# Two decoder layers on one core: one pool of eight PSUM banks, constants filled by VectorE, products of zeros at the start, and a new written-out order

## The chip, the cores and the metric

The kernel runs on one core of a Trainium2 chip. The metric is the device time in microseconds (us) of one execution. The core has TensorE (PE: matrix products, results into PSUM), VectorE (DVE), ScalarE (ACT), GpSimd (POOL) and SyncE (SP, which issues the transfers). Each engine works through its own instructions in their written order and waits for the others by semaphores. PSUM has eight banks of 512 fp32 columns in 128 partitions.

## The reference

Sixteen sequences x of 128 tokens x 128 features pass two layers, each step added to x after a layer norm without weights. `cross` takes its keys and values from `ctx`, also 128 x 128 per sequence.

```
h  = norm(x);  x += causal_attention(h, 16 heads of 8) @ Wo            # self0
h  = norm(x);  x += attention(h, ctx, 8 heads of 64) @ Wo + bo         # cross0
h  = norm(x);  x += round(h / amax(h) * 127) @ ternary(w).T * scales   # ffn
h  = norm(x);  x += causal_attention(h, scores clipped to +-10) @ Wout # self1
h  = norm(x);  x += attention(h, ctx, 16 heads of 64) @ O              # cross1
h  = norm(x);  g = softmax(h @ gate_w + gate_b); keep g >= 0.1, rescale to sum 1
               x += sum over 8 experts of g_e * (h @ W_e + b_e)        # moe
```

All is fp32. Where the kernel needs fp32 accuracy from faster products it cuts an operand into a high and a low part and adds three products.

## The kernel before, in words

The work on each sequence is cut into steps (`all_steps`, line 63), named by stage and step and numbered by sequence: `cross1.t.0#13` turns the weights of the first eight heads of the cross1 attention of sequence 13. A step lies on one engine. For one cross attention and eight heads (a unit) the chain is: `rs` (POOL, reciprocal root of the variance), `nm` (ACT, normalised rows), `xT` (PE, transposed), `xTe` (ACT, copy out of PSUM), `q` and `qe`, `s1` (PE, scores of eight heads, 1024 columns), `mx` (DVE, row maxima), `ex` (ACT, eight exponentials of 128 columns, function `cross_exps`), `rc` (DVE, reciprocal sums), `nz` (POOL, division), `t` (PE, eight transposes), `wT` (ACT, copy), `pv` (PE), `oTe` (ACT), `y` (PE), `res` (DVE, adds to x and takes the next statistics). Self attention is similar, with both units of scores written at once (`s1` or `s2`). `moe.g` is the gate, `moe.e` the experts (1024 columns). The keys (`k`) and values (`v`) of the cross attentions hang on ctx alone and are made up to six and four sequences ahead.

**Order.** No planner runs on the chip. The dictionary `ORDER` holds for each engine a string of two-letter codes, one per step: the order in which the engine does all its steps of all sequences, 721 of them on PE. The sequences are interleaved: while sequence 0 is in a late stage, others are in earlier ones. All of an engine's steps are queued behind each other.

**PSUM.** Steps that write PSUM are of two kinds. Kind X takes one bank, kind S takes two neighbouring banks (1024 columns); self scores take two such pairs. Before, four banks are for X (`X_BANKS`) and two pairs for S (`S_GROUPS`). Class `Plan` (line 258) replays the order with the steps' written costs and gives each step the bank of its kind that comes free first in that replay. This fixes the bank and the semaphore count to wait for (`room`, `room_for_scores`). The bank is free when its reader (`until`) has done all its parts.

**Array division.** `array_parts` tells how a step uses the 128 x 128 array: whole, 64 rows (cross scores), 64 columns (cross `pv`), 32 rows or 32 by 32 (self scores).

**Start.** GpSimd fills the constants (`ident`, `mask[0]`, `s_bound`, `head_rows` and small ones), shapes some by `affine_select`, and counts `consts` up. VectorE, ScalarE and TensorE wait for all of them (`N_CONSTS`) before anything else. VectorE then makes `head_mask` and `ident_b` (`const_b`). SP waits for them between its loads of `b_v` and `more`, to copy the mask into three rotated ones. The loads `e_k` and `e_v` (512 KB each, weights of cross1) are copied by ScalarE (`.hi`) and cut by GpSimd (`.lo`) before the first `cross1.k` and `cross1.v`.

Of the kernel before, what the change touches and what calls it, by code (L numbers as in the profile page):

```python
# [30 lines left out]
X_BANKS, S_GROUPS = 4, 2  # L31
AHEAD = dict(cross0=6, cross1=4)
EARLY = 4


class Step:

    def __init__(self, engine, cost, after, again, bank, until, parts, once):
        self.engine, self.cost, self.bank, self.parts, self.once = engine, cost, bank, parts, once
# [23 lines left out]
def all_steps():  # L63
    steps = {}

    def add(name, engine, cost, after=(), again=(), bank=None, until=None, parts=1, once=False):
        steps[name] = Step(engine, cost, after, again, bank, until, parts, once)
# [40 lines left out]
    def keys_values(L, chunks, k_w, v_w):  # L108
        context = ["ctx0.lo", since("ctx1.lo", EARLY)]
        for c in range(chunks):  # L110
            fill(f"{L}.k.{c}", 660, [*context, f"{k_w}.lo"], f"{L}.ke.{c}", [second_ago(f"{L}.s1.{c}", AHEAD[L])])
            add(f"{L}.ke.{c}", "ACT", 486, [f"{L}.k.{c}"])
        for c in range(chunks):
            fill(f"{L}.v.{c}", 650, [*context, f"{v_w}.lo"], f"{L}.ve.{c}", [ago(f"{L}.pv.{c}", AHEAD[L])])
# [21 lines left out]
    for name, cost in (("x0", 3300), ("first", 300), ("x1", 2300), ("c0", 400), ("b_k", 700), ("b_v", 1300),  # L136
                       ("masks", 2000), ("more", 3300), ("e_k", 1400), ("e_v", 1500), ("x", 1900), ("ctx", 2400), ("self1", 800), ("cross1", 3900), ("moe", 1300)):
        add(f"in.{name}", "SP", cost, once=True)
    add("consts", "POOL", 4150, once=True)
    for name, load, engine, hi, lo in (("ctx0", "c0", "DVE", 530, 610), ("b_k", "b_k", "DVE", 530, 610),  # L140
                                       ("b_v", "b_v", "DVE", 530, 610), ("e_k", "e_k", "POOL", 960, 1900),
                                       ("e_v", "e_v", "POOL", 960, 1900), ("ctx1", "ctx", "POOL", 1400, 2800),
                                       ("m_w", "moe", "POOL", 960, 1900)):
# [17 lines left out]
    add("moe.e", "PE", 1300, ["moe.xl", "m_w.lo"], ["moe.sm"], "S", "moe.ml")  # L161
    add("moe.lg", "DVE", 270, ["moe.g"])
# [21 lines left out]
        "aHaLaJaHa4aOa4a6a6a4a4bqaUa6aQaJbWbWbYbWbWaXaObYaLbYb0b0aHaUb2bYaQaZa6b2aJa1a4b0aXaOaZbab2aLaHb2bcaJ"  # L184
        "aUaQbea1a6b0a6aXaOaLbaaHaJaUaZbcbja1aQblbebna4aXaLa4aOa4baaZa6aHaUa1bcbwbjbyaQbeblbCaJbnbEaXbGbJbaaL"
        "aZbca1bjaHbwbebla6bybna4bQaObCbaaJbSbGa6bUbcaUa4bEbjbwaQbyblbJb6b8beaXcccabnaZbCa6claLaHa1bEbQbjbGbS"
        "chbUbwblcjbJb6byb0cab8cqbaccbnclbQbWcsbSb2aObCbcbWbYbYbGaUbEbUaJaQcqcubwchb6beaXbyb8cacsbJaZb2aLa1a4"
        "cycccjclaHcBcubja4a6bCcCbQblaObabEaJbcbnbSbGaQcGcya6cKaUbUcBcqb0becCb6csbwaXchaLcabyb8bJaHaZcGcjcccl"
        "a1cub2bWbjbWbQaOblbCbYcybnbaaUbEbGbcbYbScqcBbUaQcKaJchb0beb6cCb8aXcjbJbwaZcacscccGaLa1byclcubQbjcKb2"
        "a4aHaObCbSbEblbGbUbaaUbnaJcycqaQcBbccsbJb6aXcachb8cCaZbeaLbwa1cccjbybWclbQcubjaHbWbYbCaObScGbGblbUcy"  # L190
        "b0baaUbnbccBcqaQaJcKcCchbEb6b2becsaXb8caaLbJaZaHbwcjccclcubya4a1bja4b2bYaOblbaaJbQcGbna6cybSaQb0bcbU"
        "chbCaUcBbGbwbEcqbybecjb6cCcaaXa4aLbJaHbCb8aZcsccclbEcKa1cubjbQbWbWaOblcGbSb0bYcybnbaaUb2bUaQcBcKcqbc"
        "cCbGaJbeb6chbYbwaXb8caaLbJaHcscjclaZbycGcca1cub2bjbQa6aObCbSbaa6aJbGblcyaQbUcKbnaUbccqcBbeb0b6bEcCca"
        "chaXb8bJcjcsbwaZccclcGa1bWbycuaLbjbYbWbQaOblaHbaa6b2aJbSaUcybcbnbCaQbUcqcKbGcBbEchbeaXcCaLb0aZcsaOcj"
        "b6b0b0cabwaQb8aUclb2a1ccbycubjcGbYaXblbJaZbacybCa1bccBcqbEbnbecKcCcsbQbachb2bcbSbJcjbwcGbUbjbGbecub6"
        "byblb8cKcaccbCcyclbnbWbQbWbjbGcCcBb0bSchblbUbEcqbnbwcjcsb6bJb8bycGcacccuclbCbYbYcKbwbQbGb0bEcybSchcB"
        "bUcCcjbycqb6cGb8bJbCcacsccclcKcub2bQbEbJcybSbGbUcBchcqcCb6cjcab8bQclccbSbUcscucGb6cqb8cachcccKcyclcj"
        "cBcscCcucGchcqcjcscycBcKcucCcycBcGcKcCcGcK"
    ),
    DVE=(  # L200
        "aEaEaraEataEavaTbpaPbraEaYaTaPa2aYaTaPbfa2aEbhaTaYaPa2bfboaEaYbhaTbuaPbxaEbza2bfbobhaYbNbubKbxa2aEbf"
        "bzbobhbRaTbuaPbVbxbzbNbKaEbfaYcdbobhcmcfbRbua2bVcobxbNbzbKcdbocmbRcfcoaTaPbVbuaEbxcvbfbzaYbhbKa2bNcd"
        "cAcDcmcFcfcvcIcobRaPaTbocLcAcDbVcFbubfcIbxaEaYbhbzbNbKcdcma2cvcfcobRaTbocAaPcDbVcFbubfcLcIaYbhbKbNbx"
        "cda2cmbzcvbRcLcfcoaTaPbVaEcAbocDcFbNbKbuaYaEcIbfa2bxcdbhcmbzbRcvcocfaTbVaPcDcAbocFaEcLcIbubfaYbhbNbK"
        "cdbxcmbzcva2cocfaPbRboaTbucAbVaEcDbxcFbfbzcIaYbhbKbNcdcma2cLcfcvbRcoaTaPbocAbVcDcFcIcLbubfbxaYbhbKbN"
        "cmbzcda2cvcobRaPaTcLbVcAcfcDbobfcFcIbhaYbubNbKbxcdcmbza2cvcfcobRaTaPcAbobVcLcDcFbfaYcIbhbuaPaTbxcma2"
        "cdbzcvcoaYcfbNcAa2cDbKcFbobfcLcIbRbhbubNbKbVbxbfbzcvcLbhcdcmbocfcAbRcocDbucFbVcIbobxbNbzbKcdbucvcmcf"
        "cLbxbRcocAcDbVcFbzcIbKbNcdcmcLcvcfbRcobNbKbVcAcDcFcIbRcmcdbVcocfcvcdcLcmcfcAcDcocFcIcvcAcDcLcFcvcIcD"
# [49 lines left out]
class Plan:  # L258

    def __init__(self, steps):  # L260
# [18 lines left out]
        def begin(engine):  # L279
# [9 lines left out]
            if s.until:  # L289
                times.append(sorted(empty[s.bank].values())[len(s.until) - 1])  # L290
# [1065 lines left out]
```

## Time and profile before

| | us |
|---|---|
| median of three runs (529.69 to 532.6) | 531.2 |
| the profiled execution | 529.94 |
| its span, first to last instruction | 528.2 |

| engine | busy us | share of the span |
|---|---|---|
| PE, products | 497.7 | 94% |
| PEld, weight loads, beside the products | 419.3 | 79% |
| ACT | 441.3 | 84% |
| DVE | 409.2 | 77% |
| POOL | 395.2 | 75% |

The profile is of one execution, and its times run from the first instruction. A group "L1119 PE MATMUL S<-kT_cross,qT_cross" is line 1119, on TensorE, which writes the tile S from the two others. A row of the timeline may merge repeated instructions ("x16"): its first number is the start, its second the length in us. "Idle before" names what released the engine. The last columns of the stage view are the clock granted to TensorE (1.00 is 2.4 GHz, 0.50 is 1.2 GHz) and the load of the transfer engines.

### The profile page before, as it was taken

How to read it: one execution, taken by the hardware profiler on the slowest of the kernel's cores; microseconds unless marked ns; L12 is line 12 of the kernel's file. 1: busy time of each engine (PE TensorE's matmuls, PEld its weight loads, DVE VectorE, ACT ScalarE, POOL GpSimd, SP SyncE). 2: the span in 40 equal slices, each digit the busy share in tenths (PEclk: the TensorE clock that was granted, in tenths of full speed). 3: DMA queues.
4: the chain of work that ended last, by engine and by line, in shares of the span. 5: the costliest groups of instructions: out<-in, count | busy, mean ns of one | idle time of the engine just before them, and what ended most of it. 6: DMA issues, size and time to landing. Idle time of an engine off the chain costs nothing.

```text
span 528.2 us, 15974 instructions
## 1 busy us (share of the span) xinstructions
PE 497.7 (94%) x5490; PEld 419.3 (79%) x5490; DVE 409.2 (77%) x923; ACT 441.3 (84%) x1177; POOL 395.2 (75%) x570
## 2 busy tenths in 40 slices
PE   4998989999999999999999999999999999988884
PEld 2876777777988888788888888888988898777762
DVE  3857778887788987979788897889878887786552
ACT  5987789999888888989899888988978898887831
POOL 5785778787678987888868785898778687776454
PEclk9999999999999999999999999999999999999995
DMA  6800000000000000000000000000000000000000
GB/s 195 327 4 1 1 2 3 2 2 2 2 2 6 3 2 7 8 2 3 7 1 2 4 6 7 1 6 4 6 2 2 7 7 2 6 7 2 6 6 11
DMA packets 6463, 8.96 MB, mean 17 GB/s; under 512 B 1008, under 2 KB 4848, under 8 KB 6384
## 3 DMA queue, kind: packets, MB, share of 16 engines
q1 hardware_dynamic: 6384, 7.94, 4.6%
q8 instruction: 45, 0.74, 0.6%
q14 instruction: 34, 0.28, 0.2%
HBM read 6.50 MB, written 1.05 MB: 14 GB/s over the span
## 4 chain that ended last, share of the span: by engine, by line
PE 70%; POOL 8%; issue 7%; POOLq 6%; ACT 4%; DVE 3%; DVEq 1%; ACTq 0%
PE S L1132 11%; PE S L1119 7%; PE X L1076 7%; PE X L1159 7%; PE X L1187 7%; PE S L1106 5%; POOL diff_cross L672 4%; PE X L1292 2%; PE X L1145 2%; PE X L1198 2%; PE X L1170 2%; PE X L1172 2%; PE X L1171 2%; ACT diff_cross L747 2%; PE X L1178 2%
## 5 line engine op out<-in xcount | busy, mean ns | idle before, releaser
L667 POOL TENSOR_TENSOR w_low_self<-w_self 128x1024 f16<-128x1024 f32 x64 | 120.7, 1896 | 15.8 <-ACT w_self L736 10.9
L672 POOL TENSOR_TENSOR diff_cross<-diff_cross,e_rec_cross 128x1024 f32<-128x1024 f32 x48 | 91.0, 1898 | 24.8 <-DVE e_rec_cross L898 24.5
L747 ACT ACTIVATE diff_cross<-S,row_max_cross 128x128 f32<-128x128 f32 x384 | 103.8, 404 | 4.3 <-DVE row_max_cross L889 3.6
L889 DVE TENSOR_REDUCE row_max_cross<-S 128x8 f32<-128x1024 f32 x48 | 57.9, 1215 | 18.2 <-PE S L1119 17.7
L896 DVE TENSOR_REDUCE e_sum_cross<-diff_cross 128x8 f32<-128x1024 f32 x48 | 58.2, 1213 | 3.9 <-ACT diff_cross L747 3.2
L756 ACT ACTIVATE w_cross<-S 128x1024 f32<-128x1024 f32 x48 | 49.7, 1039 | 8.4 <-PE S L1132 8.0
L1119 PE MATMUL S<-kT_cross,qT_cross 64*128 64x128 f32 x768 | 54.6, 283 | 0.2 <-ACT qT_cross L712 0.2
L1119 PEld LDWEIGHTS S<-kT_cross,qT_cross 64*128 64x128 f32 x768 | 46.4, 187 | 7.3 <-issue 4.5
L1159 PE MATMUL X<-w_cross,v_cross 128*64 128x128 f32 x768 | 51.7, 278 | 0.1
L1132 PE MATMUL S<-ident,diff_cross 128*128 128x128 f32 x384 | 50.3, 274 | 0.9 <-POOL diff_cross L672 0.8
L1159 PEld LDWEIGHTS X<-w_cross,v_cross 128*64 128x64 f32 x768 | 41.1, 136 | 11.0 <-issue 5.7
L1132 PEld LDWEIGHTS S<-ident,diff_cross 128*128 128x128 f32 x384 | 42.8, 141 | 2.8 <-issue 1.1
L916 DVE SCALAR_TENSOR_TENSOR w_self<-S,s_bound 128x1024 f32<-128x1024 f32 x32 | 38.0, 1217 | 5.4 <-PE S L1106 5.4
L907 DVE TENSOR_TENSOR w_self<-S,row_max_self 128x1024 f32<-128x1024 f32 x32 | 39.2, 1225 | 2.4
L905 DVE TENSOR_REDUCE row_max_self<-S 128x8 f32<-128x1024 f32 x32 | 38.9, 1217 | 1.8 <-PE S L1106 1.6
L736 ACT ACTIVATE w_self<-S 128x1024 f32<-128x1024 f32 x32 | 33.0, 1032 | 7.6 <-PE S L1132 7.6
L730 ACT ACTIVATE w_self<-w_self,shift 128x1024 f32<-128x1024 f32 x32 | 36.8, 1148 | 2.8 <-DVE w_self L916 2.8
L1106 PE MATMUL S<-by_head_self,plain_self 32*128 32x512 f32 x256 | 36.5, 640 | 1.8 <-ACT by_head_self L712 1.8
L712 ACT ACTIVATE by_head_self<-X,head_mask 128x128 f32<-128x128 f32 x128 | 37.3, 402 | 0.0
L1076 PE MATMUL X<-xnT_cross,e_q 128*128 128x128 f32 x256 | 33.7, 279 | 0.7 <-issue 0.4
L1132 PE MATMUL S<-ident,w_self 128*128 128x128 f32 x256 | 33.6, 274 | 0.5 <-DVE w_self L907 0.4
L1187 PE MATMUL X<-e_o,attnT_cross 128*128 128x128 f32 x256 | 32.1, 278 | 1.5 <-issue 1.4
(191 smaller groups left out, 1396.7 us busy)
## 6 DMA issues: line engine op xcount, KB each, us to landing
out_dram<-x_all SPq DMA_DIRECT2D x16, 64.0 KB, 1.5
x_all<-in_x SPq DMA_DIRECT2D x1, 768.0 KB, 7.3
cT_all<-in_ctx SPq DMA_DIRECT2D x1, 768.0 KB, 9.0
e_k<-in_e_k SPq DMA_DIRECT2D x1, 512.0 KB, 4.9
e_v<-in_e_v SPq DMA_DIRECT2D x1, 512.0 KB, 6.0
e_q<-in_e_q SPq DMA_DIRECT2D x1, 512.0 KB, 9.0
e_o<-in_e_o SPq DMA_DIRECT2D x1, 512.0 KB, 11.3
m_w<-in_m_w SPq DMA_DIRECT2D x1, 512.0 KB, 9.0
```

Source lines behind the costliest of these rows:

```text
L667: pool.tensor_tensor(L.w_low[u][:], L.w[u][:], halves(L.w[u][:]), ALU.subtract)\
L672: pool.tensor_tensor(L.diff[u][:].rearrange("p (h k) -> p h k", h=UNIT), L.e[u][:].rearrange("p (h k) -> p h k", h=UNIT), L.e_rec[:, u, :] ...
L747: last = act.activation(L.e[u][:, P * p:P * (p + 1)], S_[:, P * p:P * (p + 1)], ACT.Exp, bias=L.row_max[:, u, p:p + 1])
L756: act.activation(L.w[u][:], group(i, turn)[:], ACT.Copy).then_inc(taken(i, turn)[0], 1)
L889: dve.tensor_reduce(L.row_max[:, u, :], group(i, turn)[:].rearrange("p (h k) -> p h k", h=UNIT), AX_X, ALU.max, negate=True).then_inc(L.ma ...
L896: dve.tensor_reduce(L.e_sum[:, u, :], L.e[u][:].rearrange("p (h k) -> p h k", h=UNIT), AX_X, ALU.add)
L1076: last = pe.matmul(bank(i, name)[:, P * k:P * (k + 1)], w[:, col:col + P], xT, start=True, stop=True)
L1106: last = pe.matmul(group(i, name, u)[:, 512 * half:512 * (half + 1)], L.plain[rows, :], L.by_head[rows, :, :].rearrange("p j n -> p (j n)" ...
L1119: last = pe.matmul(S_[:, at:at + P], L.qT[rows, h // 2, :], kT[rows, h // 2, i % 2, :], start=True, stop=True)
L1132: last = pe.transpose(S_[:, P * k:P * (k + 1)], L.diff[u][:, P * k:P * (k + 1)], ident[:])
L1159: last = pe.matmul(bank(i, name)[rows, P * pair:P * (pair + 1)], v[:, h, :], L.w[c][:, P * place(h):P * (place(h) + 1)], start=True, stop= ...
L1187: last = pe.matmul(bank(i, name)[:, 0:P], L.attnT[:, c, :], w(c), start=c == 0, stop=c == n - 1)
```

## The change

1. The eight banks are one tensor `psum`. A step of kind X takes any bank, one of kind S any two neighbours; the replay chooses those that come free first, X counting from bank 0 up and S from the top down. Each reader step has a semaphore of its own (`used_up`), and a wait that an earlier one has already covered is left out.
2. `cross_exps` counts its semaphore up after four and after eight exponentials, and the first of the two banks may be handed on after the first count.
3. VectorE fills the constants. GpSimd waits for the first four fills (`blank`), does its selections in another order and waits for all constants. VectorE waits for them behind its first statistics.
4. Before its wait for the constants, TensorE does nine products of zeros (128 x 128 by 128 x 512, bf16) into the last bank.
5. All strings of `ORDER` are new but SP's. Some written costs are changed; the consts step's goes from 4150 to 2700.

```diff
-X_BANKS, S_GROUPS = 4, 2
+BANKS = 8
+WARM = 9
-            fill(f"{L}.k.{c}", 660, ...
+            fill(f"{L}.k.{c}", 710, ...
-            fill(f"{L}.v.{c}", 650, ...
+            fill(f"{L}.v.{c}", 695, ...
-            add(f"{L}.ex.{c}", "ACT", 2060, [f"{L}.mx.{c}"], [f"{L}.t.{c}"])
+            add(f"{L}.ex.{c}", "ACT", 2060, [f"{L}.mx.{c}"], [f"{L}.t.{c}"], half=1030)
-    add("moe.e", "PE", 1300, ...
+    add("moe.e", "PE", 1385, ...
...
+        def choose(s, asked):
+            chosen, gone = [], set()
+            for _ in s.until:
+                places = range(BANKS) if s.width == 1 else range(BANKS - 2, -1, -1)
+                places = [p for p in places if not gone & {p, p + s.width - 1}]
+                since, at_ = min(((max([asked] + empty[p:p + s.width]), n) for n, p in enumerate(places)),
+                                 default=(math.inf, 0))
+                p = places[at_] if places else 0
+                gone |= set(range(p, p + s.width))
+                chosen.append((since, list(range(p, p + s.width))))
+            return chosen
...
             pool side:
-            pool.memset(ident[:], 0.0)
-            pool.memset(mask[0][:], 0.0)
-            pool.memset(s_bound[:], CLIP * SD ** 0.5)
-            pool.memset(head_rows[:], 1.0)
-            pool.drain()
+            pool.wait_ge(blank, 4)
             pool.affine_select(out=ident[:], ...
...
             cross_exps:
-                last.then_inc(taken(i, turn)[0], 1)
+                    if p % 4 == 3:
+                        last.then_inc(taken(i, turn)[0], 1)
...
             VectorE, in self0.st of sequence 0, after the statistics:
+                        dve.wait_ge(consts, N_CONSTS)
+                        dve.tensor_reduce(head_mask[:], ...).then_inc(const_b, 1)
+                        dve.tensor_copy(ident_b[:], ident[:]).then_inc(const_b, 1)
             and ahead of all its steps:
-            dve.wait_ge(consts, N_CONSTS)
+            dve.memset(ident[:], 0.0).then_inc(blank, 1)
+            dve.memset(head_rows[:], 1.0).then_inc(blank, 1)
+            dve.memset(mask[0][:], 0.0).then_inc(blank, 1)
+            dve.memset(s_bound[:], CLIP * SD ** 0.5).then_inc(blank, 1)
+            dve.memset(weighted[:, 4:8, :], 0.0).then_inc(still_ready, 1)
+            dve.memset(eps[:], LN_EPS)
...
             TensorE:
+            def room(i, name):
+                for j, user, half in plan.before[i, name]:
+                    count = use_count(j, user, half)
+                    if waited.get(user, 0) < count:
+                        pe.wait_ge(used_up[user], count)
+                        waited[user] = count
...
+            pe.wait_ge(still_ready, 1)
+            for _ in range(WARM):
+                pe.matmul(psum[:, 512 * (BANKS - 1):512 * BANKS], still[:, 0:P], still[:, 0:512], start=True, stop=True)
             pe.wait_ge(consts, N_CONSTS)
```

Two passages of the order that the prediction speaks of. PE from its first step on: before `xT#0 v#0 qk#0 xT#1 cross0.k.0#0 self0.s1#0`, after `xT#0 v#0 qk#0 cross0.k.0#0 cross0.k.0#1 cross0.k.0#2 xT#1 self0.s1#0` (self0's steps where no stage is named). ACT near the end: before `cross1.ex.0#13 cross1.ex.1#13 self1.qke#15`, after `cross1.ex.0#13 self1.qke#15 cross1.ex.1#13`.

## Rows read from the trace of the kernel before

**Rows 1.** The page, part 1: busy us (share of the span) and instructions.
```profile
PE 497.7 (94%) x5490; PEld 419.3 (79%) x5490; DVE 409.2 (77%) x923; ACT 441.3 (84%) x1177; POOL 395.2 (75%) x570
```
**Rows 2.** Busy us by stage: PE, PEld, DVE, ACT, POOL, clock, DMA, GB/s.
```profile
35.00:125.00 90.00, 84.34 (x950) 67.27 (x949) 69.35 (x145) 76.81 (x201) 69.30 (x105) 1.00 0.01 2
125.00:450.00 325.00, 324.37 (x3704) 279.02 (x3702) 271.60 (x619) 289.37 (x788) 253.93 (x360) 1.00 0.02 4
450.00:500.00 50.00, 44.06 (x491) 36.31 (x490) 35.00 (x81) 40.33 (x115) 32.93 (x42) 1.00 0.02 6
500.00:529.00 29.00, 17.51 (x113) 13.42 (x113) 12.59 (x48) 8.05 (x24) 14.44 (x20) 0.79 0.03 8
```
**Rows 3.** Timeline of the start: start us, length us, what.
```profile
0.92 0.53 POOL L609 MEMSET mask<- 128x512 bf16 x1
1.53 0.11 POOL L611 MEMSET head_rows<- 128x16 f32 x1
...
3.35 0.20 POOL L622 TENSOR_SCALAR_AFFINE_SELECT head_rows<-head_rows 128x16 f32<-128x16 f32 x1
4.04 0.16 POOL L631 MEMSET v_self<- 128x32 f32 x1
...
5.08 0.19 POOL L638 TENSOR_TENSOR var_eps_self<-mean_var_self,eps 128x1 f32<-128x1 f32 x1 [0.89 <-DVE mean_var_self L860]
7.15 0.45 PE L1292 MATMUL X<-ident,xn_self 128*128 128x128 f32 x1 [7.15 <-ACT xn_self L762]
```
**Rows 4.** Timeline of TensorE in the middle, and its last cross1.xT.
```profile
202.06 1.16 PE L1119 MATMUL S<-kT_cross,qT_cross 64*128 64x128 f32 x16
203.16 0.33 PE L1292 MATMUL X<-ident,xn_cross 128*128 128x128 f32 x1
...
299.18 1.09 PE L1159 MATMUL X<-w_cross,v_cross 128*64 128x128 f32 x16
300.20 2.06 PE L1119 MATMUL S<-kT_cross,qT_cross 64*128 64x128 f32 x32
302.19 0.71 PE L1198 MATMUL X<-xnT_self,d_qk 128*128 128x128 f32 x4
...
355.89 1.97 PE L1159 MATMUL X<-w_cross,v_cross 128*64 128x128 f32 x32
357.79 0.33 PE L1292 MATMUL X<-ident,a_unit 128*128 128x128 f32 x1
...
489.52 0.33 PE L1292 MATMUL X<-ident,xn_cross 128*128 128x128 f32 x1 [0.27 <-ACT xn_cross L762]
```
**Rows 5.** Transfers: size, us from issue to landing.
```profile
x_all<-in_x SPq DMA_DIRECT2D x1, 64.0 KB, 2.0
e_k<-in_e_k SPq DMA_DIRECT2D x1, 512.0 KB, 4.9
```
**Rows 6.** Timeline of TensorE, products of 256 columns, early and late.
```profile
10.10 0.42 PE L1171 MATMUL X<-cT_all_lo,b_k_hi 128*128 128x256 f32 x1
10.32 0.41 PE L1172 MATMUL X<-cT_hi,b_k_hi 128*128 128x256 f32 x1
...
156.28 0.28 PE L1171 MATMUL X<-cT_all_lo,b_k_hi 128*128 128x256 f32 x1
156.40 0.28 PE L1172 MATMUL X<-cT_hi,b_k_hi 128*128 128x256 f32 x1
```
**Rows 7.** Timeline: issue of e_k, its low part, its first product.
```profile
10.57 0.43 SPq L595 DMA_DIRECT2D e_k<-in_e_k  x1
...
16.81 2.39 POOL L559 TENSOR_TENSOR e_k_lo<-e_k,e_k_hi 128x1024 fp32r<-128x1024 f32 x1 [0.52 <-ACT e_k_hi L773]
19.42 0.36 PE L1170 MATMUL X<-cT_hi,e_k_lo 128*128 128x256 f32 x1
```
**Rows 8.** Timeline of ScalarE near the end.
```profile
465.35 4.25 ACT L747 ACTIVATE diff_cross<-S,row_max_cross 128x128 f32<-128x128 f32 x16
```
**Rows 9.** Waits, 450 to 500 us: us in total, times, longest.
```profile
PEld S L1106 <- ACT by_head_self L712: 1.8, 1, 1.8
```

More of the change, by code:

```diff
@@ L64, in all_steps, with add @@
     steps = {}
-    def add(name, engine, cost, after=(), again=(), bank=None, until=None, parts=1, once=False):
-        steps[name] = Step(engine, cost, after, again, bank, until, parts, once)
+    def add(name, engine, cost, after=(), again=(), bank=None, until=None, parts=1, once=False, half=0):
+        steps[name] = Step(engine, cost, after, again, bank, until, parts, once, half)
     def fill(name, cost, after, until, again=(), parts=1, once=False):
@@ L189 @@
[L189 to L193, printed above, removed]
@@ L306, in __init__ @@
             ended[i, name] = now + cost + TAIL[engine]
-            for k in range(len(s.until)):
-                b = min((since, b) for b, since in empty[s.bank].items())[1]
-                empty[s.bank][b] = math.inf
-                self.bank[i, name, k] = b
-                self.turn[i, name, k] = (turns[s.bank][b], turns[s.bank][b] + s.parts)
-                turns[s.bank][b] += s.parts
+            self.before[i, name] = []
+            for k, (_, chosen) in enumerate(choose(s, now)):
+                self.banks[i, name, k] = chosen
+                for b in chosen:
+                    if last[b]:
+                        self.before[i, name].append(last[b])
+                    empty[b] = math.inf
             if name in gives:
                 taken, k = gives[name]
-                empty[steps[taken].bank][self.bank[i, taken, k]] = ended[i, name] + HOP[engine]["PE"]
+                for z, b in enumerate(self.banks[i, taken, k]):
+                    half = s.half and z == 0
+                    empty[b] = now + (s.half if half else cost) + TAIL[engine] + HOP[engine]["PE"]
+                    last[b] = i, name, bool(half)
         self.end = max(ended.values())
@@ L436, in bank @@
         def bank(i, name):
-            return X[plan.bank[i, name, 0]]
+            b = plan.banks[i, name, 0][0]
+            return psum[:, 512 * b:512 * (b + 1)]
         def gates(i, k):
@@ L443, in group, with use_count @@
         def group(i, name, k=0):
-            return S[plan.bank[i, name, k]]
+            b = plan.banks[i, name, k][0]
+            return psum[:, 512 * b:512 * (b + 2)]
+        def use_count(i, user, half=False):
+            s = plan.steps[user]
+            if s.half:
+                return 2 * i + (1 if half else 2)
+            return readers[user] * (i + 1)
+        readers = {u: s.parts for s in plan.steps.values() for u in s.until}
         def emptied(i, name):
-            return x_free[plan.bank[i, name, 0]], plan.turn[i, name, 0][1]
+            user = plan.steps[name].until[0]
+            return used_up[user], use_count(i, user)
         def taken(i, name, k=0):
-            return s_free[plan.bank[i, name, k]], plan.turn[i, name, k][1]
+            user = plan.steps[name].until[k]
+            return used_up[user], use_count(i, user)
         x_all = sb("x_all", [P, NSEQ, P])
@@ L1083, in self_scores1 @@
                 pe.wait_ge(*emptied(i, f"{L.name}.qk"))
-                room_for_scores(i, name, 2)
+                room(i, name)
                 if i == 0:
```

171 lines of the change are left out of this document (85 added, 86 removed).

## The prediction

> **What bounds the kernel now.** I read the page's engine table first, then the busy time by stage, the start times of TensorE's products, the start of the timeline, and the waits last. The page puts TensorE's products at 94% of the span and the other engines between 75% and 84% [rows 1], so TensorE is the bound, with little room around it. By stage the reader is to see a middle (125 to 450 us) with 324.4 us of 325 busy, a filling stretch before it (35 to 125) with 5.7 us of 90 idle, and a drain from 450 with 17.4 us of 79 idle [rows 2]; in front lies a start whose first product comes at 7.15 [rows 3].
>
> Busy time hides short gaps, because a product's end is modelled and overlaps the next start. So I counted from start to start. On an undisturbed TensorE a step costs about: keys 0.71 and values 0.72 us (48 each), cross projection 0.89 (48), cross scores 1.0 (48), a turn of eight blocks 0.87 (80), weights times values 0.92 (48 cross) and 0.81 (32 self), self scores 1.29 and 0.92 (16 each), experts 1.47 (16), cross output 0.89 and 1.77 (16 each), the 289 small steps together 51. The sum is 452 us. Each change of the array's division (whole, 64 rows, 64 columns, 32 rows) adds about 0.1: a cross score group that stands alone takes from 202.06 to 203.16, 1.10 us, while two together take 300.20 to 302.19, 1.99 instead of 2.20; a group of weights times values alone takes 299.18 to 300.20, 1.02, and two take 355.89 to 357.79, 1.90 instead of 2.04 [rows 4]. Joining two groups saves two changes, so one is worth 0.07 to 0.105. PE's order string holds 204 of them, 21 us. TensorE thus has 473 us of work in a span of 528.2. The lag (start of a step minus the work that stands before it in the order) tells where the rest goes: it is 9.7 us at 35 us, 22.7 at 123, 30.9 at 451, and 50 at TensorE's end, 523, with 5 of tail behind. Filling costs 13 us, the middle 8, the drain 19.
>
> The Trainium skill would read more headroom into the middle. Its page "Perfetto Trace Analysis", section "Identifying the Most-Contended Engine", says that matmul busy time is a bad measure of the distance to the limit and that the busy share of weight loads is one to use; by that the middle stands at 86% (279.0 of 325 us), and an order could win up to 45 us there. The values above, which repeat step after step, say that only 8 are to be had. I go by the starts.
>
> **The change, part by part.** The profiled execution took 529.9 us for a span of 528.2 and lies 1.3 us under the median of 531.2. The terms are worked out on it and carried over to the median.
>
> *Constants by VectorE.* Today GpSimd makes all of them and the last ends at 4.20; its first reciprocal root starts at 5.08, the first product at 7.15. After, VectorE clears four tiles; GpSimd ended the same four at 1.64, I take 1.7. GpSimd's selections ended at 3.55 [rows 3], so they should end at 3.4. VectorE's other fills lie beside them: one of 512 columns at 0.53 (the mask's row), two of 128 columns and seven tiny ones at about 0.9 together, done near 3.1. The first statistics no longer wait for constants but for x, 2.0 us from issue to landing [rows 5], about 3.0. GpSimd can then start near 3.75 instead of 5.08, and the first transposed product could start at 5.8. The wait for all constants now stands in VectorE's queue behind the first statistics and holds the second ones and the cuts; the cuts wait for ScalarE's copies anyway, so it costs nothing. Were the constants made in another order than I think, it costs up to 0.5.
>
> *Products of zeros.* TensorE has nothing else before 5.8. The granted clock is printed as 1.00 from the start, but the early products run at the lower of the two levels, 1.2 GHz: 256 columns are 0.22 us apart at 10.10, and 0.12 apart at 156.28 [rows 6]. TensorE had worked from 7.15 before it rose, near 11.3. At 1.2 GHz nine products of 512 columns take 9 x 0.43 = 3.9 us. They start when VectorE has filled their operand, near 2.4, and end at 6.3: that is half a microsecond after the first real product could come, so that one starts at 6.3 and not 7.15. In exchange the key products before the first scores cost 0.71 and not 1.4 us. The key weights should be cut at 8.9; three key steps then lie before the first scores, which start at 11.2 as now, but with 3.3 us of work done instead of 1.75. The lag falls by 1.5. If the zeros do not raise the clock it falls by 0.5; at best, with data alone as the limit, by 2.5.
>
> *New order at the start.* Much of this meets a load. e_k lands 4.9 us after its issue [rows 5], which is at 10.57, so at 15.5; its low part is ready at 19.20, and the first product with it starts at 19.42 [rows 7]: 0.2 us of cover. SP's wait ahead of the mask copies ended with the constants at 4.20 and had just begun then (its issues before it fill its queue to 4.0), so e_k leaves only 0.2 us earlier and its low part is ready at about 18.9. The new order has 10.5 us of work ahead of it, not 9.75, so the lag there is 8.4 against 9.7. I take **1.3 us** for the whole start (0.3 to 2.5).
>
> *New order, changes of division.* The new string holds 185 against 204. 19 x 0.1 = **1.9 us** (1.3 to 2.0 by the two pairs), all on the bounding engine.
>
> *One pool; a score group's first bank handed on at half time.* ScalarE reads a cross score group in eight activations, 2.1 us (sixteen in 4.25 [rows 8]); the first four free one bank after 1.05. It can then take any single product, and turns, scores and experts can use any two neighbours. TensorE's work stays the same. The 48 more increments lie on ScalarE, which idles 36 us in the middle [rows 2]; I price them at nothing, and at 48 x 0.1 = 5 us at most if that idle time were gone. How much of TensorE's stall is waiting for banks the trace does not tell apart; the whole stall of the middle is 8 us, so the gain there is 0 to 6. The new step costs for keys, values and experts (710, 695, 1385 ns instead of 660, 650, 1300) stand nearer to the measured 710, 720 and 1470, so the planned times by which banks are dealt out drift less. I take **0.5** for the middle, and **1.0** of the 13 in filling (minus 4 to plus 6: the order is new throughout and nothing in the trace fixes it).
>
> *New order, drain.* One stall can be named: the last self scores wait 1.8 us for ScalarE, which stands in sixteen exponentials from 465.35 to 469.6 ahead of copying that sequence's queries and keys [rows 8, 9]. In the new order eight of them come after. From the last cross1.xT on (489.52 [rows 4]), 21.8 us of work are left in both orders under a chain of 38.7 us, so nothing is won there. I take **1.3** (minus 1 to plus 5).
>
> Sum: 1.3 + 1.9 + 0.5 + 1.0 + 1.3 = 6.0 us. 529.9 becomes 523.9, and the median of 531.2 becomes **525.2**.
>
> **Rivals.** (a) *Only what can be counted comes:* the start is eaten at e_k (0.3), the changes give 1.9, everything else returns as other stalls: 529.0. For it: filling and drain are latency of one sequence's chain over four engines, which banks do not shorten. (b) *The order is much better:* filling and drain give 5 and 4 us, the middle 1.5, the start 2, the changes 1.9, together 14.4: 516.8. For it: 32 us of stall outside the middle; against it: the untouched tail. (c) *Slower, by pairs of banks.* Scores had two pairs of their own. Now a pair is free only when both neighbours are, and one bank can be held long: the gate's until VectorE has normalised its weights. The dealing follows planned times, so a late reader stops TensorE with everything queued behind. A pair is taken 176 times; if each waits 0.07 us more on average, 12 us are lost beside the 6 won: 537. From 0.034 us each on, nothing is won. Against it: the other engines idle 11 to 22% in the middle and so keep near the plan [rows 2]. (d) *The change does not do what it says:* zeros do not raise the clock, and the order only moves stalls: 531.
>
> **How the numbers follow.** Chances: forecast 0.46, (a) 0.20, (b) 0.13, (c) 0.13, (d) 0.08. A difference under 0.5%, 2.7 us, cannot be told from none here. Faster (under 528.5): the forecast's 0.46, four tenths of (a), all of (b), together 0.67. Slower: most of (c), 0.12. Within: the rest, 0.21. The range of 518 to 532 leaves out half of (b) and most of (c), 0.17; the forecast's own range is 521.5 to 528.5.
>
> **What the profile after would show.** Nine products of zeros from about 2.4, 0.43 apart; the first real product near 6.3, and key products 0.12 apart from the first one on. The first product with e_k's low part at 18.9. A lag of 8.4 us at 35, 20.4 at 123 and 28.1 at 451, over 471 us of work. No wait over 0.5 us of the last self scores for ScalarE. I am wrong if score steps in the middle stand behind long waits for one bank's last reader, if the zeros end after 7.15, or if the chain from the last cross1.xT to the end grows beyond 38.7 us.

## The result and the profile after

| us | before | after |
|---|---|---|
| median of four runs each | 530.73 (529.69 to 532.6) | 517.82 (516.53 to 520.02) |
| the profiled execution | 529.94 | 516.53 |
| its span | 528.2 | 514.5 |

The ratio is 0.976, interval 0.974 to 0.979: 12.9 us less, where 6.0 were forecast (5.5 against this median). The time is 7.4 us under the forecast and 0.2 us under the range. Rival (b), "the order is much better", had said 516.8.

Part 1 of the page of the changed kernel, the line that answers to [rows 1]:
```profile
PE 491.8 (96%) x5499; PEld 417.4 (81%) x5499; DVE 409.7 (80%) x937; ACT 440.0 (86%) x1177; POOL 393.6 (77%) x557
```
TensorE's busy time fell by 5.9 us although nine products came in; the other engines do what they did. By stage, as [rows 2]:
```profile
35.00:125.00 90.00, 86.98 (x1040) 70.37 (x1037) 72.55 (x150) 80.80 (x217) 70.07 (x105) 1.00 0.01 2
125.00:450.00 325.00, 323.36 (x3707) 281.10 (x3706) 276.07 (x639) 291.30 (x794) 260.13 (x369) 1.00 0.02 4
450.00:500.00 50.00, 44.95 (x490) 38.98 (x489) 33.81 (x85) 38.44 (x105) 32.62 (x41) 1.00 0.02 6
500.00:529.00 29.00, 5.53 (x18) 3.29 (x16) 5.30 (x17) 1.89 (x7) 6.79 (x11) 0.80 0.02 5
```
The reader is to see two things. In filling TensorE starts 1040 products where it started 950. And after 500 us 5.5 us of products are left instead of 17.5: by then the kernel is 12 us ahead. The middle shows next to nothing by busy time, so the lag (start of a step minus the work ahead of it in its own order) is taken again, for both kernels at the first step from 35, 124 and 452 us on. The last stretch holds all that is left of the span.

| us | before | after | gain | forecast |
|---|---|---|---|---|
| lag at 35 | 9.7 | 9.0 | 0.7 | 1.3 |
| filling, 35 to 124 | 13.0 | 8.5 | 4.5 | 1.0 |
| middle, 124 to 452 | 8.6 | 6.2 | 2.4 | 0.5 |
| drain and tail | 23.8 | 19.5 | 4.3 | 1.3 |
| work with changes of division | 473.1 | 471.3 | 1.8 | 1.9 |
| span | 528.2 | 514.5 | 13.7 | 6.0 |

The steps themselves cost what they cost before (a turn 0.873 us in both middles, an experts step 1.47); the work differs by the 19 changes alone. The 1.8 us for them are those 19 at the cost that the rows of before give for one, about 0.1 us; no run measures them by themselves.

The start after, on three engines, in the columns of [rows 3]:
```profile
0.88 0.17 DVE L1085 MEMSET ident<- 128x128 f32 x1 [0.88 <-PEq L1391]
...
1.07 0.27 DVE L1087 MEMSET mask<- 128x256 uint32 x1
...
2.08 4.02 PE L1350 MATMUL psum<-weighted 128*128 128x512 bf16 x9 [2.08 <-DVE weighted L1089]
...
3.56 0.19 POOL L661 TENSOR_TENSOR var_eps_self<-mean_var_self,eps 128x1 f32<-128x1 f32 x1 [0.23 <-DVE mean_var_self L884]
...
5.89 0.42 PE L1331 MATMUL psum<-ident,xn_self 128*128 128x128 f32 x1
...
6.77 0.46 PE L1246 MATMUL psum<-a_v,xnT_self 128*128 128x128 f32 x2 [0.46 <-ACT xnT_self L735]
...
8.80 0.36 PE L1209 MATMUL psum<-cT_hi,b_k_lo 128*128 128x256 f32 x1 [1.12 <-DVE b_k_lo L590]
...
9.00 0.28 PE L1210 MATMUL psum<-cT_all_lo,b_k_hi 128*128 128x256 f32 x1
9.12 0.28 PE L1211 MATMUL psum<-cT_hi,b_k_hi 128*128 128x256 f32 x1
```
The zeros start at 2.08, GpSimd's first root at 3.56, the first real product at 5.89 and the first key product at 8.80, and behind that first one the key products are 0.12 apart, where they were 0.22 apart before [rows 6]: the higher clock is there. The low part of e_k is met as foreseen, 0.4 us earlier than before [rows 7]:
```profile
16.49 2.36 POOL L590 TENSOR_TENSOR e_k_lo<-e_k,e_k_hi 128x1024 fp32r<-128x1024 f32 x1 [4.03 <-ACT e_k_hi L797]
...
18.98 0.36 PE L1209 MATMUL psum<-cT_hi,e_k_lo 128*128 128x256 f32 x1
```
The end: TensorE's last cross1.xT, which stood at 489.52 [rows 4], and from the view of waits from 450 to 500 us the wait that answers to [rows 9]:
```profile
477.01 0.27 PE L1331 MATMUL psum<-ident,xn_cross 128*128 128x128 f32 x1
```
```profile
PEld psum L1145 <- ACT by_head_self L735: 0.9, 1, 0.9
```
From the last cross1.xT to the end it is 37.5 us against 38.7. The named wait fell from 1.8 to 0.9. ScalarE's sixteen exponentials in one piece [rows 8] are gone. The same two groups, of sequence 13, now have the queries and keys of sequence 15 between them, and stand some 10 us earlier:
```profile
455.10 2.18 ACT L770 ACTIVATE diff_cross<-psum,row_max_cross 128x128 f32<-128x128 f32 x8
457.12 0.33 ACT L735 ACTIVATE plain_self<-psum 128x128 f32<-128x128 f32 x1
457.29 1.19 ACT L735 ACTIVATE by_head_self<-psum,head_mask 128x128 f32<-128x128 f32 x4
458.29 2.25 ACT L770 ACTIVATE diff_cross<-psum,row_max_cross 128x128 f32<-128x128 f32 x8
```

### The profile page after: what moved, and what is told of

Same layout as the page of the kernel before. It is cut to its first block, busy times and chain, and to the rows that moved or that the text cites. A ratio compares the mean times of both kernels' runs of the same rounds, so it can differ in the third digit from the quotient of the medians.

```text
span 514.5 us, 15998 instructions
## 1 busy us (share of the span) xinstructions
PE 491.8 (96%) x5499; PEld 417.4 (81%) x5499; DVE 409.7 (80%) x937; ACT 440.0 (86%) x1177; POOL 393.6 (77%) x557
## 4 chain that ended last, share of the span: by engine, by line
PE 77%; ACT 7%; issue 4%; DVE 4%; POOLq 3%; POOL 3%; DVEq 1%; DMA 0%; ACTq 0%
PE psum L1171 12%; PE psum L1158 9%; PE psum L1198 8%; PE psum L1226 8%; PE psum L1115 8%; PE psum L1145 5%; PE psum L1184 3%; PE psum L1331 2%; PE psum L1237 2%; ACT diff_cross L770 2%; PE psum L1217 2%; PE psum L1186 2%; PE psum L1218 2%; PE psum L1219 2%; PE psum L1209 2%
## 5 line engine op out<-in xcount | busy, mean ns | idle before, releaser
L770 ACT ACTIVATE diff_cross<-psum,row_max_cross 128x128 f32<-128x128 f32 x384 | 104.5, 410 | 7.9 <-DVE row_max_cross L913 7.4
L913 DVE TENSOR_REDUCE row_max_cross<-psum 128x8 f32<-128x1024 f32 x48 | 58.0, 1218 | 17.8 <-PE psum L1158 17.7
L780 ACT ACTIVATE w_cross<-psum 128x1024 f32<-128x1024 f32 x48 | 49.9, 1049 | 6.0 <-PE psum L1171 5.1
L1158 PE MATMUL psum<-kT_cross,qT_cross 64*128 64x128 f32 x768 | 53.2, 282 | 0.5 <-ACT qT_cross L735 0.3
L1198 PEld LDWEIGHTS psum<-w_cross,v_cross 128*64 128x64 f32 x768 | 41.1, 136 | 15.4 <-issue 13.7
L1198 PE MATMUL psum<-w_cross,v_cross 128*64 128x128 f32 x768 | 51.3, 278 | 0.3 <-issue 0.2
L1158 PEld LDWEIGHTS psum<-kT_cross,qT_cross 64*128 64x128 f32 x768 | 46.0, 187 | 6.4 <-issue 4.2
L1171 PE MATMUL psum<-ident,diff_cross 128*128 128x128 f32 x384 | 49.3, 273 | 0.4 <-ACT by_head_self L735 0.3
L1171 PEld LDWEIGHTS psum<-ident,diff_cross 128*128 128x128 f32 x384 | 42.7, 141 | 1.7 <-ACT by_head_self L735 0.5
L931 DVE TENSOR_TENSOR w_self<-psum,row_max_self 128x1024 f32<-128x1024 f32 x32 | 39.2, 1225 | 2.4
```

What stands on the lines that cost most here:

```text
L770: last = act.activation(L.e[u][:, P * p:P * (p + 1)], S_[:, P * p:P * (p + 1)], ACT.Exp, bias=L.row_max[:, u, p:p + 1])
L780: act.activation(L.w[u][:], group(i, turn)[:], ACT.Copy).then_inc(taken(i, turn)[0], 1)
L913: dve.tensor_reduce(L.row_max[:, u, :], group(i, turn)[:].rearrange("p (h k) -> p h k", h=UNIT), AX_X, ALU.max, negate=True).then_inc(L.ma ...
L1158: last = pe.matmul(S_[:, at:at + P], L.qT[rows, h // 2, :], kT[rows, h // 2, i % 2, :], start=True, stop=True)
L1171: last = pe.transpose(S_[:, P * k:P * (k + 1)], L.diff[u][:, P * k:P * (k + 1)], ident[:])
L1198: last = pe.matmul(bank(i, name)[rows, P * pair:P * (pair + 1)], v[:, h, :], L.w[c][:, P * place(h):P * (place(h) + 1)], start=True, stop= ...
```

## The experiments

Theory: the gain is the new order, and it comes only with the banks and the dealing for which that order was laid out. Rivals: the pool by itself gives it; the start gives it; the order gives it whatever the banks are. The last could not be tried directly: the new order asks for more banks at once than four single ones and two pairs offer (replayed with those, it comes to a stop), so an order was searched for those banks instead (below). Times are medians, ratios are to the kernel before in the same job (530.4 to 531.0 us), with 95% intervals.

| kernel | banks | order | start | us | ratio |
|---|---|---|---|---|---|
| after | pool, half | new | new | 517.8 | 0.976 |
| e1 | pool, half | old | new | 537.5 | 1.012 [1.009, 1.015] |
| e5 | pool, half | old | old | 536.0 | 1.011 [1.008, 1.014] |
| e6 | 4 and 2 pairs | old | new | 532.3 | 1.003 [1.002, 1.005] |
| e3 | pool, half | new | old | 517.4 | 0.974 [0.972, 0.977] |
| e8 | pool, no half | new | new | 532.9 | 1.004 [1.002, 1.006] |
| e9 | pool, half, dealt by the old costs | new | new | 523.1 | 0.986 [0.984, 0.989] |
| e10 | 4 and 2 pairs | searched | new | 526.8 | 0.992 [0.989, 0.995] |
| e15 | 4 and 2 pairs | e10's | 11 zeros more | 525.0 | 0.990 [0.988, 0.991] |
| e12 | pool, half | searched | new | 520.9 | 0.982 [0.980, 0.983] |
| e14 | pool, half | e12's | 11 zeros more | 518.5 | 0.977 [0.976, 0.979] |
| e11 | pool, no half | searched | 5 zeros more | 517.8 | 0.976 [0.975, 0.978] |
| e16 | pool, half | new | 5 zeros more | 516.8 | 0.974 [0.973, 0.976] |

The same account of the lag, each from one profiled execution:

| us | lag at 35 | filling | middle | drain, tail | work | span |
|---|---|---|---|---|---|---|
| e1 | 9.2 | 15.7 | 8.4 | 27.0 | 473.1 | 533.4 |
| e5 | 11.5 | 16.6 | 8.5 | 24.5 | 473.1 | 534.2 |
| e6 | 11.1 | 12.9 | 9.0 | 24.1 | 473.1 | 530.2 |
| e3 | 11.4 | 8.7 | 5.7 | 18.5 | 471.3 | 515.6 |
| e8 | 10.3 | 9.8 | 18.1 | 22.4 | 471.3 | 531.9 |
| e9 | 11.1 | 9.1 | 10.3 | 20.0 | 471.3 | 521.8 |
| e15 | 12.7 | 9.3 | 6.5 | 21.6 | 472.6 | 522.7 |
| e11 | 9.7 | 7.7 | 7.0 | 19.6 | 471.2 | 515.2 |
| e16 | 9.6 | 8.4 | 6.4 | 18.8 | 471.3 | 514.5 |

### The old order over the new banks

e1 is the changed kernel with the strings of before; e5 has the old start as well. Both deal the banks by the new costs.

```diff
-        "aHaLaJa4a4a4aHaOa4a6a6a6a6aQaJbqaUbYbYbWbYbYaX...
+        "aHaLaJaHa4aOa4a6a6a4a4bqaUa6aQaJbWbWbYbWbWaXaO...
```

> The kernel after with the order strings of before; pool, half-time hand-on, fills by VectorE, zeros and new costs kept. Theory A (the new order makes the gain; the pool only allows it): 528 to 531 us, the 1 to 2 us of the start are all that is left. Rival B (the pool frees TensorE from bank waits in any order): 519 to 522. By A the lag (start of a TensorE step less the work before it) goes from 9.7 at 35 us to over 21 at 123, by B to 18.

> Order and start of before, the pool of eight banks, half-time hand-on and new costs alone. Theory A: no gain, 530 to 532 us. Rival B: 520 to 523 us. If it is slower than 534, the dealing of banks by planned times does harm by itself under an order that was not laid out for it.

Measured: 537.5 and 536.0, both slower than before by more than their intervals. Without its order the pool does not help: the kernel is 5 to 6.5 us slower, about the 537 of rival (c) of the prediction. Part of it is that rival's mechanism, waits for banks, in filling. TensorE's waits from 35 to 125 us (waited for, total, times, longest), first the kernel before, then e1:
```profile
PE X L1217 <- DVE attn_self L934: 0.8, 2, 0.4
```
```profile
PE psum L1145 <- DVE attn_self L958: 1.9, 1, 1.9
PE psum L1171 <- ACT diff_cross L770: 1.2, 1, 1.2
```
The first row is the largest item of the kernel before in this stretch. In e1 self scores wait once, 1.9 us, for VectorE to have read another step's output (`attn_self`), and a turn of weights 1.2 us for the exponentials of a score group: neither uses the waiting step's own data, so what they wait for is a bank. The middle loses nothing (8.4 against 8.6).

Another part is the clock. The last self scores of e1 come behind a wait of 1.62 us for their own data, about the wait that the kernel before has at the same place. In e1 the granted clock falls to 0.50 there, from 474.6 to 481.4 us; before, it does not. In e5 it falls from 82.7 to 86.1, at the end of the bank wait of 1.95 us. The same eight score products, first in the kernel before, then in e1 and e5:
```profile
470.85 1.14 PE L1106 MATMUL S<-by_head_self,plain_self 32*128 32x512 f32 x8 [1.64 <-ACT by_head_self L712]
```
```profile
474.06 1.64 PE L1145 MATMUL psum<-by_head_self,plain_self 32*128 32x512 f32 x8 [1.62 <-ACT by_head_self L735]
```
```profile
82.83 2.09 PE L1141 MATMUL psum<-by_head_self,plain_self 32*128 32x512 f32 x8 [1.95 <-DVE attn_self L969]
```
At the lower level the products take nearly twice as long (2.09 us for 1.14). By estimate, 6.8 us at that level cost e1 up to 3.4 us, as much as its drain loses (27.0 against 23.8), and 3.4 us of it cost e5 up to 1.7 of the 3.6 us that its filling loses. So what banks alone cost the old order is shown for filling only, 2.7 us in e1. The rest of the 5 to 6.5 us is in good part lost clock, in one case behind a bank wait and in the other not.

### The new order without the hand-on at half time, and with the old dealing

```diff
e8:
-            add(f"{L}.ex.{c}", "ACT", 2060, ..., half=1030)
+            add(f"{L}.ex.{c}", "ACT", 2060, ...)
-                    if p % 4 == 3:
-                        last.then_inc(taken(i, turn)[0], 1)
+                last.then_inc(taken(i, turn)[0], 1)
e9:
-            fill(f"{L}.k.{c}", 710, ...
+            fill(f"{L}.k.{c}", 660, ...
-            fill(f"{L}.v.{c}", 695, ...
+            fill(f"{L}.v.{c}", 650, ...
-    add("moe.e", "PE", 1385, ...
+    add("moe.e", "PE", 1300, ...
```

> The kernel after with one edit: a cross score group's two banks are handed on together, after its eighth exponential. Order and pool stay; the banks are dealt out anew. Theory A2 (order and bank dealing fit each other; an order in banks it was not laid out for loses): 523 to 532 us. Rival D (the order's steps are good in themselves, and one bank a microsecond later is small): 518 to 520 us.

> The kernel after, but the banks are dealt out by the old costs of keys, values and experts (660, 650, 1300). Only bank numbers and the waits for them change. Theory A2: 520 to 524 us, since a dealing by other times sends steps to banks whose reader is late. Rival D: 517 to 519 us, no change.

e8 gives back all of the gain, 15.1 us over after, with 48 increments fewer to do. 12 of its 17.4 us of span are lost in the middle, where busy time now shows it (up to 1.7 of the 12, by estimate, are a fall of the clock from 127.8 to 131.2, behind a wait of 1.75 us for exponentials):
```profile
125.00:450.00 325.00, 315.39 (x3580) 271.30 (x3578) 265.07 (x606) 281.45 (x763) 248.96 (x355) 0.99 0.02 4
```
One such place in the timeline of e8, the experts of sequence 0:
```profile
151.34 0.24 DVE L896 TENSOR_TENSOR moe_lo<-psum,moe_hi 128x128 fp32r<-128x128 f32 x1
...
153.54 2.19 ACT L770 ACTIVATE diff_cross<-psum,row_max_cross 128x128 f32<-128x128 f32 x8
...
153.73 0.39 PE L1301 MATMUL psum<-m_g,moe_xnT 128*128 128x8 f32 x2
...
155.87 0.47 PE L1312 MATMUL psum<-m_w_hi,moe_lo 128*128 128x512 f32 x1 [1.75 <-ACT diff_cross L770]
```
The experts' data (`moe_lo`) have been there since 151.58. TensorE does the gate at 153.73 and then stands for 1.75 us until the eight exponentials of another sequence have read their two banks. In the changed kernel the same two steps follow each other:
```profile
146.85 0.39 PE L1302 MATMUL psum<-m_g,moe_xnT 128*128 128x8 f32 x2
147.09 0.48 PE L1313 MATMUL psum<-m_w_hi,moe_lo 128*128 128x512 f32 x1
```
e9 changes no instruction of the work, only which bank each step gets (157 of 721 differ) and the waits for them, and costs 5.3 us. Of the 7.3 us of its span, 4.1 are in the middle (10.3 against 6.2) and 2.1 before 35 us, where self scores stand for a bank whose reader is late:
```profile
PE psum L1130 <- DVE attn_self L958: 1.6, 1, 1.6
```
Costs of three kinds of steps that are 45 to 85 ns lower are enough for that.

### The start

e3 is the changed kernel with the start of before. e6 has the new start under the old order and the old kinds of banks. It is not the new start alone: it deals the banks by the new costs, and in the replays of the two kernels 331 of the 721 banks taken come from another step than before.

```diff
-WARM = 9
+WARM = 0
-            pool.wait_ge(blank, 4)
+            pool.memset(ident[:], 0.0)
+            pool.memset(mask[0][:], 0.0)
+            ...
```

> The kernel after with the start of before: GpSimd makes all constants, every engine waits for them first, no products of zeros. Theory A: the start gives what is still there at 35 us, 0.65 us of lag, and what later stages keep of it: 518 to 520 us. Rival C (the early start is carried through to the end and multiplies, since each engine's chain of sequence 0 begins earlier): 521 us or more.

> Order of before, four single banks and two pairs as before, no half-time hand-on; only the start of after (fills by VectorE, zeros) and the reader's semaphores. Theory A: 529 to 530.5 us. Rival C: 527 or less. My prediction's term for the start was 1.3 us: 529.4.

e3 takes 517.4 (517.2 to 517.4 in four runs): in the median the new start gives nothing (0.5 us the other way, inside the intervals). Its profiled lag at 35 us is 2.4 higher than after's, as a start without zeros should be. Of that 1.0 comes back in the drain (18.5 against 19.5), and its executions are all alike, while those of after spread over 3.5 us: it is 0.3 to 0.8 us slower than after's two short ones. e6 is 1.3 us slower than before, and whether by its start or by its dealing stays open. TensorE's timeline in e6:
```profile
2.08 4.02 PE L1349 MATMUL psum<-weighted 128*128 128x512 bf16 x9 [2.08 <-DVE weighted L1088]
5.90 0.42 PE L1330 MATMUL psum<-ident,xn_self 128*128 128x128 f32 x1
7.74 0.77 PE L1245 MATMUL psum<-a_v,xnT_self 128*128 128x128 f32 x2 [1.42 <-ACT xnT_self L735]
...
9.88 0.42 PE L1209 MATMUL psum<-cT_all_lo,b_k_hi 128*128 128x256 f32 x1
10.10 0.41 PE L1210 MATMUL psum<-cT_hi,b_k_hi 128*128 128x256 f32 x1
...
14.04 0.28 PE L1209 MATMUL psum<-cT_all_lo,b_k_hi 128*128 128x256 f32 x1
14.16 0.28 PE L1210 MATMUL psum<-cT_hi,b_k_hi 128*128 128x256 f32 x1
```
The same nine zeros, at the same time. Here the key products are still 0.22 apart at 10.10 and the rise comes at 14.0, later than near 11.5 in the kernel before, without zeros. Between the zeros and the keys TensorE waited 1.42 us for a copy (0.46 in after). That alone does not decide it: e1, with the same start, the same first steps and a wait of 1.25 us at the same place, is at the higher clock from 7.0 on:
```profile
7.56 0.46 PE L1246 MATMUL psum<-a_v,xnT_self 128*128 128x128 f32 x2 [1.25 <-ACT xnT_self L735]
...
9.61 0.28 PE L1210 MATMUL psum<-cT_all_lo,b_k_hi 128*128 128x256 f32 x1
9.72 0.28 PE L1211 MATMUL psum<-cT_hi,b_k_hi 128*128 128x256 f32 x1
```
Nor is the time of the rise fixed without zeros: e5 starts with the same products as the kernel before, within 0.02 us, and its clock rises at 14.4, not 11.5. In ten of the eleven kernels with zeros at the front the clock rises at 4.9 to 8.1 us, in the three without them at 11.5 to 14.4. So zeros at the front mostly bring the early rise, but not each time, and why e6 missed it stays open.

### Orders searched for other banks

To see whether the old banks could have had this gain, orders were searched: neighbouring steps exchanged in the engines' strings, kept where a replay with the given banks and step costs becomes shorter. e10 is for four banks and two pairs with whole groups and was searched from the old order; e12, for the pool with the hand-on at half time, and e11, for the pool with whole groups, were searched from the new one. They are three finds of such a search, not the best orders there are.

```diff
e10, e15:
-                places = range(BANKS) if s.width == 1 else range(BANKS - 2, -1, -1)
+                places = range(4) if s.width == 1 else (6, 4)
e10, e15, e11:
-            add(f"{L}.ex.{c}", "ACT", 2060, ..., half=1030)
+            add(f"{L}.ex.{c}", "ACT", 2060, ...)
e14 and e15 (11), e11 and e16 (5), behind sequence 0's v and qk:
+                    for _ in range(11):
+                        pe.matmul(psum[:, 512 * (BANKS - 1):512 * BANKS], still[:, 0:P], still[:, 0:512], ...)
all but e16: new strings in ORDER
```

> Four single banks and two pairs as before, no half-time hand-on, start and new costs of after, and an order of my own: searched from the old one by moving single steps, for exactly these banks. 198 changes of division. Theory A3 (a better order is not to be had without the pool): 525 to 530 us. Rival E (before was just badly searched, the pool is not needed): 517 to 521 us.

> The kernel after with my own order, searched from its order with start-to-start costs as measured in the trace (keys 714, values 712, experts 1465, self scores 1285 and 920, a change of division 95 or 150 ns). 194 changes. If order and costs are what counts (A2), it beats after: 508 to 514 us. If not (D), 516 to 520.

Both came out with a cold stretch at the start. TensorE in e12:
```profile
6.68 0.61 PE L1237 MATMUL psum<-xnT_self,a_qk 128*128 128x128 f32 x4
9.80 0.66 PE L1130 MATMUL psum<-mask,ident_b 32*32 32x512 bf16 x16 [2.51 <-DMA mask<-mask]
10.39 2.09 PE L1145 MATMUL psum<-by_head_self,plain_self 32*128 32x512 f32 x8
...
15.14 0.38 PE L1209 MATMUL psum<-cT_hi,b_k_lo 128*128 128x256 f32 x1
15.35 0.28 PE L1210 MATMUL psum<-cT_all_lo,b_k_hi 128*128 128x256 f32 x1
```
The queries and keys of sequence 0 ran at the higher level (0.61 us for four products, as in after). Then TensorE waits 2.5 us for the copied mask, as this order has no key steps to do before the scores. The granted clock falls at 8.5, and the scores take 2.09 us where e16 needs 1.14. The clock is back at 15.3. In e10 it is back at 19.0, and its runs spread from 523.3 to 527.8. So zeros were put into that gap, and the question of the banks was asked again with this disturbance gone:

> e12_search_costs with eleven more products of zeros (0.22 us each at the upper clock level) on TensorE behind sequence 0's first v and qk, where that kernel idled 2.5 us; its clock had risen at 5.1 us, fallen at 8.5 and risen again only at 15.3. Theory F (my searched order lost to after by the clock of its first 15 us, not by its order): 516.0 to 518.0 us, 3 to 4 less than e12. Rival G (it lost by bank waits all along): 520 to 521 us.

> e10_search_split (four single banks and two pairs, order searched for them) with the same eleven products of zeros; its clock rose for good only at 19.0 us. Theory A3 (the pool is needed for the rest): 521 to 524 us. Rival E (before was only badly searched): 517 to 519 us.

> Pool of eight banks, groups handed on whole, an order searched for exactly that from after's order, and five more products of zeros in the first gap. e8, the same banks under after's order, took 532.9 us. Theory A2 (an order fitted to its banks is what counts; the half-time hand-on itself is small): 518 to 522 us. Rival H (the half-time hand-on is itself worth most of the 15 us that e8 lost): 527 us or more.

e15, the best found for the old banks, is 5.5 us faster than before. e11 and e14, for the pool, are 12.7 and 12.1 us faster. So at least 5.5 us of the gain are order that the old banks could have had. The other 7 are at most what the pool adds, for e10's search began at another order than e11's. The account says where they lie (e15 against e11): 3.0 up to 35 us, 1.6 in filling, 2.0 in the drain, 1.4 in fewer changes of division, and nothing in the middle. The 3.0 up to 35 us need not be the banks' doing: the kernel before, with the same kinds of banks, has a lag of 9.7 there, as e11 has, against e15's 12.7. That leaves about 4 us that the pool may be needed for, which is argued from the account, not shown by a run. e11 also settles the hand-on at half time. Taken away under an order that counts on it, it costs 15 us; with an order made for whole groups, at most 1 us is missing (517.8, against 517.8 of the changed kernel and 516.8 of e16, which has e11's five more zeros).

### The changed kernel with five more zeros

> The kernel after with five more products of zeros behind sequence 0's first v and qk, in its idle stretch from 7.7 to 8.8 us. Its four runs had been 516.5, 517.0, 518.6 and 520.0 us, the first two with a mean clock of 0.991, the others 0.983 to 0.985. Theory F: all executions now have the early clock, 516.3 to 517.3 us with less spread. Rival: the spread is not the clock's, 517.8 us as after, or 0.3 more by the added products.

516.8 us (516.55 to 517.08 in four runs), against 516.5 to 520.0 without them. It is the fastest kernel here by median, 1.0 us under after, though the two ratios' intervals overlap (0.973 to 0.976, 0.974 to 0.979), and none of its four executions was one of the longer ones. TensorE's timeline in e16:
```profile
8.10 1.24 PE L1333 MATMUL psum<-weighted 128*128 128x512 bf16 x5
9.13 0.36 PE L1209 MATMUL psum<-cT_hi,b_k_lo 128*128 128x256 f32 x1
9.33 0.28 PE L1210 MATMUL psum<-cT_all_lo,b_k_hi 128*128 128x256 f32 x1
...
11.92 1.14 PE L1145 MATMUL psum<-by_head_self,plain_self 32*128 32x512 f32 x8
```
They push the first key product from 8.80 to 9.13 and raise the lag at 35 us by 0.6. In exchange, so far as the times tell, the clock is kept in all four.

## Why the prediction was wrong

*Right.* The bound, TensorE, and where its stall lay. Every step's own cost is unchanged, and the changes of division are the 19 that were counted. The start in its single times: root at 3.56 (3.75), first real product 5.89 (6.3), keys at 8.8 (8.9) and 0.12 apart, first use of e_k's low part at 18.98 (18.9). The named wait, under 1 us if not under the 0.5 I set. None of the three signs of being wrong appeared (the zeros ended before 7.15, the chain at the end shrank to 37.5 us, no score step of the middle stood long for a bank), and the forecast was wrong all the same: they watched for a loss, and what was missed is a gain.

*Wrong, the sizes of three terms.* Filling was taken at 1.0 and gave 4.5; drain at 1.3 and gave 4.3; the middle at 0.5 and gave 2.4. The step that failed is the one by which they were priced. I took pool, half-time hand-on, costs and order as separate edits, looked for a row that shows each one's stall, found one (1.8 us), and put a small number on what no row shows. The runs show that they are one edit: the same new order gives 12.9 us with its banks and its dealing, 7.3 with the old dealing (e9) and minus 2.5 without the hand-on (e8), and the same pool gives minus 5 to minus 6.5 with the old order (e1, e5). A sum over the parts, each priced by itself, does not give 12.9. The lag shows it by place: 8.4, 20.4 and 28.1 us were foreseen at 35, 123 and 451, and 9.0, 17.5 and 23.7 came.

*Wrong, the reason against.* For rival (a) I wrote that filling and drain are latency of one sequence's chain, which banks do not shorten. Filling fell by a third. Even the order searched for the old banks has 9.3 us of it for 13.0, and the one searched for the pool 7.7. The stall was the interleaving, which an order can change, and only the last part was chain: from the last cross1.xT on 1.2 us are won, as foreseen (nothing). The other 3.1 of the drain come before that product: the lag at it was 38.2 (7 more than at 452) and is 27.5 (4 more), by the same 21.8 us of work behind it.

*Wrong, what the start is worth.* The single times were right, and the lag at 35 us shows 0.7 instead of 1.3. But e3 without any of it is as fast in the median. The prediction took the rise as something that the zeros bring. In the traces the same nine zeros are followed by a rise at 4.9 to 8.1 us in ten kernels and at 14.0 in an eleventh, so it mostly came; but a clock that has risen can fall again behind a wait (e1, e5, e8, e10, e12). The two longer executions of after have a lower mean granted clock, 0.985 and 0.983 against 0.991 in the two short ones. For the longest, a mean lower by 0.008 over 518 us is some 8 us more at 0.50 instead of 1.00, which costs about 4 us by estimate, and it is 3.5 us longer: the clock accounts for its length. Where that clock was lost no trace shows. That no such execution came with five more zeros speaks for the start; four executions are few, and in e1, e5 and e8 the falls lie elsewhere.

*The rivals.* (b) came, with sizes near its own (filling 5, drain 4, middle 1.5, changes 1.9) but for the start (2). The one thing against it was the untouched tail, and from the last cross1.xT on only 17 of the 55 us of stall are lost, so its chance of 0.13 was low for the reason given. (c) is real in its mechanism: bank waits in filling under the old order (e1), and the experts' wait in e8. Its size of 5 us and more is reached under the old order only together with lost clock. What keeps it away in the changed kernel is that the order was laid out with the banks (e9, e8). Of (d), zeros that do not raise the clock are seen in e6's first 14 us alone.

What stays open: how the gain would divide under the best orders for each set of banks, since the searched ones are finds from different beginnings, and how often the clock is lost in each kernel, since there is one trace of each.

## What to carry to other kernels

When a written-out order and the buffers under it change together, price them as one: a good order spends every bank at the moment it comes free, so the same buffers under another order, or the same order under slightly different release times, can be slower than where one started (here by 2.5 to 6.5 us, with 5 to 20 us between kernels that share most of the change). Take the total stall outside the steady state as what the pair can win, and give a large share of it a real chance, even if no single wait is long: 45 us lay in filling, middle and drain, and the longest wait that I could name in them was 1.8. Look at the granted clock before a loss is put down to waits: a wait can cost its own length and, behind it, slower products. Zeros in a gap right ahead of the first heavy products are worth a try beside those at the front; here the pair was at most 1 us better than zeros at the front alone.

## What the runs showed of the hardware

With the nine zeros at the same 2.08 us in each of eleven kernels, the granted clock rose at 4.9 us (e8), 6.6 (after), 7.0 (e1), 8.1 (e9) and, in the others but e6, between these times; in e6 it rose at 14.0. e1 and e6 begin with the same steps. Without zeros it rose at 11.5 (before), 12.8 (e3) and 14.4 (e5); before and e5 begin with the same steps at the same times. The time of the rise is thus no property of the order alone.

In e10 and e12 it rose near 5.2, fell at 8.7 and 8.5 within 2.7 and 2.5 us without a product, and was back at 19.0 and 15.3. In full work it fell for 3.4 us at the end of a wait of 1.95 us (e5) and right behind one of 1.75 us (e8, at 127.8), and for 6.8 us behind one of 1.62 us (e1). Waits of the same length were followed by no fall in the kernel before (1.64 us, 470.85), in e1 (1.94 us, 80.25) and in e8 (1.75 us, 155.87). At the front, the profile's clock column prints 1.00 even where the products run at the lower level (e6's stretch from 8 to 13 us): the distance of repeated products, 0.22 or 0.12 us for 256 columns, is what to read.

VectorE cleared the mask as 256 words of 32 bits in 0.27 us; GpSimd had taken 0.53 for the same tile [rows 3].
